# Feed-forward up products of an audio tower: from one product in full fp32 to three products of split halves

## The reference

```
h = tok(x)                                  # projection, layer norm, 5-tap conv with soft gates, W_ff, relu
h = h + attn(layernorm(h), w_qkv, w_o)      # 8 heads of 64
h = h + ffn(layernorm(h), up, down, perm)

def ffn(x, up, down, perm):                 # up [16, 64, 256], down [16, 256, 64]
    t = x.reshape(b * l, 1024)[:, perm].reshape(b * l, 16, 64)
    t = einsum('bhd,hdm->bhm', t, up)       # the up products: K is 64
    t = gelu(t, approximate=False)
    t = einsum('bhm,hmd->bhd', t, down)     # the down products: K is 256
    return t.reshape(b * l, 1024)[:, unperm]
```

## Time and profile before

| | us |
|---|---|
| median of 3 runs | 996.25 (995.29 to 996.93) |
| the profiled execution, its time | 1000.3 |
| the same, span from first to last instruction | 997.8 |
| PE busy | 959.8 (96%) |
| DVE busy | 507.4 (51%) |
| ACT busy | 426.6 (43%) |
| POOL busy | 401.4 (40%) |
| feed-forward stage, first up product to end of span | 860.0 to 997.8 |

### The profile page before, as it was taken

How to read it: one execution, slowest core, us unless ns; L and a number is a source line. 1 busy time by engine, 2 the same in 40 slices (tenths; PEclk the granted TensorE clock), 3 DMA queues, 4 the chain that set the end, 5 groups by cost and what they waited for, 6 DMA issues and landing times.

```text
span 997.8 us, 15717 instructions
## 1 busy us (share of the span) xinstructions
PE 959.8 (96%) x6108; PEld 713.8 (72%) x6108; DVE 507.4 (51%) x841; ACT 426.6 (43%) x756; POOL 401.4 (40%) x324
## 2 busy tenths in 40 slices
PE   7999999999999799999999999999999999999996
PEld 5777878777777688788778878878887877533331
DVE  6144444478545610454466256257154468759451
ACT  6144444464552542444444244234232232467553
POOL 1124242435651113535352352342023278668632
PEclk9899999999999999999999999999999999999999
DMA  8550908286345225418300300200024976724521
GB/s 287 199 203 1 184 34 176 61 151 170 127 138 153 92 43 162 139 64 302 120 11 12 106 2 21 106 1 22 29 81 157 265 264 235 272 92 127 175 79 63
DMA packets 74919, 122.87 MB, mean 123 GB/s; under 512 B 29143, under 2 KB 38359, under 8 KB 70878
## 3 DMA queue, kind: packets, MB, share of 16 engines
q1 hardware_dynamic: 68686, 104.93, 35.0%
q0 software_dynamic: 5120, 16.78, 4.9%
q10 hardware_dynamic: 1040, 0.16, 0.1%
HBM read 79.36 MB, written 42.50 MB: 122 GB/s over the span
## 4 chain that ended last, share of the span: by engine, by line
PE 79%; DVE 5%; POOL 5%; issue 4%; ACT 3%; DMA 2%; SPq 0%; POOLq 0%; ACTq 0%; DVEq 0%
PE bank L333 20%; PE bank L334 19%; PE bank L335 19%; PE bank L1848 6%; PE bank L1857 6%; POOL vacc L369 2%; DMA stage<-w_proj 2%; POOL wf_l L327 2%; DVE yr_l L1197 2%; PE bank L1600 2%; DVE sq L414 1%; ACT sq L419 1%; PE bank L1730 1%; PE bank L435 1%; ACT yr_h L857 1%
## 5 line engine op out<-in xcount | busy, mean ns | idle before, releaser
L369 POOL TENSOR_TENSOR vacc<-vacc,sq 128x512 f32<-128x512 f32 x72 | 96.8, 1344 | 41.6 <-ACT sq L419 28.3
L333 PE MATMUL bank<-xa_h,wp_h 128*128 128x512 f32 x256 | 104.1, 406 | 7.1 <-DVE xa_l L1148 7.1
L333 PE MATMUL bank<-cv_h,wf_h 128*128 128x512 f32 x256 | 104.9, 410 | 4.1 <-DVE lg L1212 2.4
L334 PE MATMUL bank<-xa_l,wp_h 128*128 128x512 f32 x256 | 101.8, 398 | 0.0
L335 PE MATMUL bank<-xa_h,wp_l 128*128 128x512 f32 x256 | 101.7, 397 | 0.0
L334 PE MATMUL bank<-cv_l,wf_h 128*128 128x512 f32 x256 | 100.5, 393 | 0.0
L335 PE MATMUL bank<-cv_h,wf_l 128*128 128x512 f32 x256 | 100.4, 392 | 0.0
L1129 ACT ACTIVATE gt<-bank 128x512 f32<-128x512 f32 x128 | 66.2, 602 | 54.1 <-PE bank L1848 54.0
L735 POOL TENSOR_TENSOR fo<-fo,res 128x512 f32<-128x512 f32 x32 | 42.3, 1337 | 112.6 <-ACT fo L881 69.6
L1848 PE MATMUL bank<-dd,up_f 64*128 64x512 f32 x256 | 64.9, 625 | 0.4 <-ACT gt L1129 0.4
L397 POOL TENSOR_TENSOR acc<-acc,ho 128x512 f32<-128x512 f32 x24 | 34.2, 1424 | 72.4 <-ACT ho L852 70.1
(11 more groups left out here) (178 smaller groups left out, 2173.7 us busy)
## 6 DMA issues: line engine op xcount, KB each, us to landing
xs<-x_t SPq DMA_DIRECT2D x32, 256.0 KB, 6.2
h_s<-ho SPq DMA_DIRECT2D x8, 1024.0 KB, 5.0
res<-h_s SPq DMA_DIRECT2D x32, 256.0 KB, 3.6
h_s<-fo SPq DMA_DIRECT2D x32, 256.0 KB, 2.4
dc<-h_s SPq DMA_DIRECT2D x4, 2048.0 KB, 8.9
h<-h_s SPq DMA_DIRECT2D x8, 1024.0 KB, 8.1
h_s<-h SPq DMA_DIRECT2D x8, 1024.0 KB, 5.3
band_s<-zero SPq DMA_DIRECT2D x4, 1072.0 KB, 8.5
```

Of the source, the lines that this page charges most:

```text
L333: pe.matmul(o, wh, xh, start=start, stop=False)
L334: pe.matmul(o, wh, xl, start=False, stop=False)
L369: g.tensor_tensor(vacc[:, :], t[:, 0, :] if k == 1 else vacc[:, :], t[:, at, :], ALU.add).then_inc(ln_vac, 1)
```

## The change

The operands of the up products are split as those of the other stages, and `ff_up` makes three passes.

- `up` is loaded raw; ACT makes its high part in two copies of 128x1024 and DVE the low part in place, in two subtractions, both at the end of o chunk c = 2.
- Each block of the input gets a high part from ACT (`xd_high`, in a ring of RING = 4 tiles), three steps ahead, behind the gelus of a step, and a low part from DVE (`xd_low`) that overwrites the scaled block, two steps ahead, behind `d_add`. DVE makes the low parts of blocks 0 and 1 in the o stage, ahead of its last two evacuations.
- `ff_up` now has six float32r products for each `blk` where it had two in float32, and waits for `xd_lo` in place of `xd_sc`.
- Two semaphores are added (`xd_hi`, `xd_lo`), and the ring of raw weight loads goes from 9 to 7.

```diff
-        up_f = place("up_f", [P, KB, FF_MID], F32, R1)
+        up_h = place("up_h", [P, KB, FF_MID], F32R, R1)
+        up_r = place("up_r", [P, KB, FF_MID], F32, R1 + 8 * KIB)
+        up_l = place("up_l", [P, KB, FF_MID], F32R, R1 + 8 * KIB)
+        dd_h = place("dd_h", [P, RING, N], F32R, STAGE)
+        dd_l = place("dd_l", [P, KB, N], F32R, R2 + 48 * KIB)
...
+                if c == CH - 2:
+                    act.wait_ge(up_ld, 32)
+                    for i in range(2):
+                        act.activation(up_h[:, 4 * i:4 * i + 4, :], up_r[:, 4 * i:4 * i + 4, :], ACT.Copy).then_inc(w_hi, 1)
+            def xd_high(b):
+                act.wait_ge(xd_sc, b + 1)
+                if b >= RING:
+                    act.wait_ge(up_mm, 4 * (b - RING) + 4)
+                act.activation(dd_h[:, b % RING, :], dd[:, b % KB, :], ACT.Copy).then_inc(xd_hi, 1)
+            for b in range(RING - 1):
+                xd_high(b)
...
                 gelus(s // KB, s % KB)
+                if s + RING - 1 < CH * KB:
+                    xd_high(s + RING - 1)
...
+            def xd_low(b):
+                v.wait_ge(xd_hi, b + 1)
+                v.tensor_tensor(dd_l[:, b % KB, :], dd[:, b % KB, :], dd_h[:, b % RING, :].bitcast(F32),
+                                ALU.subtract).then_inc(xd_lo, 1)
...
                     o_low(c + 1, range(PAIRS - 1))
+                else:
+                    xd_low(0)
+                    xd_low(1)
                 o_evac(c, A_GROUPS[2])
...
+                if c == CH - 2:
+                    for i in range(2):
+                        half = slice(4 * i, 4 * i + 4)
+                        v.wait_ge(w_hi, U_END + i + 1)
+                        v.tensor_tensor(up_l[:, half, :], up_r[:, half, :], up_h[:, half, :].bitcast(F32),
+                                        ALU.subtract).then_inc(w_lo_v, 1)
...
                     d_add((s - 1) // KB, (s - 1) % KB)
+                if s + 2 < CH * KB:
+                    xd_low(s + 2)
...
-                    since(pe, xd_sc, c, 8, a + 1)
+                    since(pe, xd_lo, c, 8, a + 1)
...
+                b = (8 * c + a) % RING
                 for j, r in enumerate(halves):
-                    mm = pe.matmul(bank[2 * blk + j][:, :], up_f[r, a, cols], dd[r, a, :], start=True, stop=True)
+                    pe.matmul(bank[2 * blk + j][:, :], up_h[r, a, cols], dd_h[r, b, :], start=True, stop=False)
+                for j, r in enumerate(halves):
+                    pe.matmul(bank[2 * blk + j][:, :], up_h[r, a, cols], dd_l[r, a, :], start=False, stop=False)
+                for j, r in enumerate(halves):
+                    mm = pe.matmul(bank[2 * blk + j][:, :], up_l[r, a, cols], dd_h[r, b, :], start=False, stop=True)
...
-            pe.wait_ge(up_ld, 32)
+            pe.wait_ge(w_lo_v, lo_before[0][U_END] + 2)
...
+RING = 4
+
-RAW = 9
+RAW = 7
```

More of the change, by code:

```diff
@@ L205, in audio_tower @@
         d_ld, d_cent = [sem(f"d_ld{i}") for i in range(2)], sem("d_cent")
-        xd_sc, up_ld = sem("xd_sc"), sem("up_ld")
+        xd_sc, xd_hi, xd_lo, up_ld = (sem(s) for s in ("xd_sc", "xd_hi", "xd_lo", "up_ld"))
         g_ld = [[sem(f"g_ld{i}{k}") for k in range(KB)] for i in range(2)]
@@ L649, in _ @@
             for s in range(2):
-                sp.dma_start(up_f[FF_IN * s:FF_IN * (s + 1), :, :],
+                sp.dma_start(up_r[FF_IN * s:FF_IN * (s + 1), :, :],
                              up.rearrange("(a s) d m -> s d a m", s=2)[s]).then_inc(up_ld, 16)
```

## The result

The changed kernel takes 1001.29 us (median of 20 runs, 996.95 to 1008.48), the kernel before in the same comparison 996.48 (20 runs). The ratio is 1.0049, 95% interval 1.0032 to 1.0067: slower by 4.9 us where 4.9 less was forecast. The prediction was wrong in sign. One run far slower than all others, of 1347.28 in experiment 8, is left out of its times.

A forecast was written before the change was run, and what follows sets the result against it. PE was taken as the bound, with less room in steps 8 to 14. Terms -11.5 + 3.3 + 0.4 + 1.6 + 1.3 = -4.9 took 996.25 to 991.4, overall range 987 to 998.5.

The forecast's parts named there:

- the clock: Behind the variance product: left unchanged; a second half-clock stretch at the start would cost 1.7, chance 0.07 with DVE's waits.
- the ring: Smaller ring of weight loads: last load and `c_load(1)` 2.3 later, costing PE about 1.3, nothing more at POOL's sum; bounds 0 and 4.
- the table loads: Behind ACT's two table loads in the feed-forward a copy stands in front of the gelus, costing 0.4.
- The up products: Feed-forward on PE: six slots of 0.227 a step, each step saves 0.36, 32 steps save 11.5.
- Rival 1: Every slot of `ff_up`: float32r weight loads at 64 rows not hidden, nothing saved, time 999.2; chance 0.11.
- Steps 15 to 31 all have this length: Kernel before, feed-forward on PE: each of these steps takes 3.78.
- ACT: High copies in the feed-forward: 0.3 behind per step with squares, costing nothing alone but leaving no room for DVE's lateness.
- DVE against POOL: Steps 8 to 13: DVE's low parts, held by POOL's additions, give back 3.3 to PE; bounds 0 and 5.
- The pass of 3.8: DVE in steps 8 to 11: six operations and a short wait take 3.8 a step, before POOL's holds.
- the five holds of 0.95: Steps 8 to 13: POOL's additions hold DVE five times for about 0.95 each.
- rival 2: DVE, POOL, start and ring give back nearly all, only the steps behind 15 gain; time 996, chance 0.20.
- The start: Start of the feed-forward: low parts ahead of the last evacuations make PE begin 1.6 later; bounds 0.7 and 3.7.

The follow-up runs named there:

- experiment 8: Changed kernel with ring of nine, blocks 6 and 7 prepared later, last centrings spread out and their mean read from PSUM; ratio 0.9991, 995.4.
- 9: The ceiling: changed kernel with ring of nine, no low part of the blocks on DVE, second pass reading the high part; ratio 0.9920, 8.0 under before.
- 2: The ring-of-nine kernel: changed kernel with the ring of raw weight loads back at nine; ratio 1.0029, +2.9 against the kernel before.
- experiment 10: Changed kernel with ring of nine, POOL's additions for the last two variances on 8 of 512 columns; ratio 0.9932, 989.5.
- psum_center: The kernel of experiment 6: changed kernel with ring of nine, last eight centrings reading their mean from PSUM; ratio 0.9996, 995.9.
- best2: Changed kernel with ring of nine, both variances' centrings reading the mean from PSUM, DVE's start reordered with blocks 6 and 7 in steps 0 and 1; 0.9950, 991.3.
- 7: Kernel before (ring of nine, float32 up products) with the blocks' copies, subtractions and PE's waits added, results unused; ratio 1.0072, +7.2.
- 3: Changed kernel (ring of seven) with the last centrings spread over steps 8 to 14 and the variance product moved to step 16; ratio 1.0039, +3.9.
- 5: Changed kernel with ring of nine, low parts of blocks 0 and 1 ahead of the evacuations, blocks 6 and 7 prepared behind them; ratio 1.0010, +1.0.
- experiment 6: Same run as psum_center: changed kernel with ring of nine, last eight centrings reading their mean from PSUM instead of SBUF; ratio 0.9996, 995.9.
- 4: Changed kernel (ring of seven) without DVE's low parts for blocks 2 to 31, the second pass reading the high part; ratio 0.9974, 993.7.
- experiment 1: Kernel before with only the ring of raw weight loads cut from nine to seven; ratio 1.0032, +3.2.

## Why the prediction was wrong

Two steps of the prediction failed. It put the clock at nothing ("I leave this as it is"), where the feed-forward has 10.2 us at half clock for 3.4 before, up to 3.4 us of cost, and the ring another stretch of 3.4, up to 1.7. And it put the low parts beside POOL at 3.3, where PE's waits behind the start sum to 5.3. At full clock the feed-forward was to be 6.2 shorter (-11.5 + 3.3 + 0.4 + 1.6) and is 1.8 shorter.

By measured times the 4.9 are -8.0 for the products (9), +10.9 for what the low parts do to DVE and the clock (from 9 to 2), +2.0 for the ring (from 2 to the changed kernel), each within about 3. Forecast were -11.1 (with the table loads), +4.9 and +1.3.

- **The up products: right in mechanism, 0.9 too much in size.** The slot is 0.232 instead of 0.227, a step saves 0.33, 32 steps 10.6. Rival 1 is dead: loads of 64 rows are hidden. ("Steps 15 to 31 all have this length" holds from 16 on; step 15 of before took 5.43, with the stretch of the earlier trace rows in it, which changes no sum.) The 8.0 of the ceiling is less, since there too PE waits.
- **ACT: right, but for a path that it left out.** ACT's copies beside the squares cost PE nothing in experiment 10, as forecast. What PE waits for in the ceiling (1.3 for gelus) is DVE's preparation, held by POOL and handed on through ACT's order: a high copy that waits 1.91 for its block holds the gelus behind it. The changed kernel has it too (0.58 at 908.50, there through a square that waits 1.50 for a centring), and psum_center (1.71 and 0.62) and best2 (1.42 and 0.63) have it most. The prediction said that ACT "leaves no room for DVE's lateness" and gave about 1 for squares; the copy as a second such place isn't in its sum.
- **DVE against POOL: right in mechanism, 2.0 too small.** Behind the start PE waits 0.48 + 0.71 + 0.58 + 1.53 + 2.02 = 5.3 in the changed kernel, over the 3.3 forecast and over its bound of 5. The pass of 3.8 was right (3.74 without POOL's time), the five holds of 0.95 weren't: in steps 9 to 11 a hold lasts 1.5, a whole POOL addition, in every pass, and the passes take 5.2 to 5.7. Experiments 7 and 10 settle it: 5.24 with PE's old step, 3.74 without POOL's time. PE can't gain anything where DVE's pass is longer than even its old step and DVE's lead is used up, and steps 1 to 4 were so too (passes of 4.0 to 4.5), which I had left out: the waits of 0.48 and 0.71 stand right behind them. Experiments 3, 5 and 8 show that order alone moves the waits and doesn't remove them. Removing the second SBUF input (6) frees the centrings, yet at full clock that is worth 0.7, because the preparation and low parts are held in their place; removing POOL's time (10) removes the waits.
- **The clock: put at nothing, and the larger error in kind.** "I leave this as it is; a second such stretch at the start would cost 1.7" was put with rival 2's waits into a rest of 0.07, 998 to 1000, the forecast nearest to what came. The ring-of-nine kernel has 10.2 of half-clock in the feed-forward, the ceiling 0; over all their runs the difference is 10.0. That is 3.1 to 5.1 of the 10.9, by the two prices above. Every profiled kernel that waited 1.9 to 2.6 for a low part ahead of its first up product (after, 2, 3, 4, 6, 10) had a stretch of 3.4 or 6.8 right behind it; 5, 8, 9 and 11, which wait under 0.4 there, had none, nor 1 with 1.0 and 7 with 1.3. PE's waits for DVE were priced at their own length, and not at what the clock does behind them.
- **The start: 1.6 forecast, 2.7 in the trace of after** (3.0 between the stages against 0.32), 1.9 with the ring of nine. Within its bounds.
- **The ring: mechanism right, size off.** `c_load(1)` is 2.5 later (2.3 forecast), PE loses 2.2 and not 1.3 in experiment 1, since POOL's sum was late by 1.1 on top, which I had ruled out. In the changed kernel it is 2.4, all of it in the one gap of 2.18 and what follows it directly, with nothing added at POOL's sum. Why the same delay splits in one kernel and not in the other is open.
- **Rival 2 had the right shape** (nearly all given back, by DVE, POOL, start and ring), but ended at 996, for want of the clock.

The Trainium skill ("SBUF — State Buffer", section "SBUF: two separate sides") says that the lock between DVE and POOL holds for a DVE operation with two SBUF inputs against a POOL operation that reads SBUF. Experiment 6 agrees: with one input in PSUM no centring was held, 0.69 or less, where the same centrings had taken 2.1. I had used the rule for the price of a hold, but not to ask which operations hold whom.

What stays open: why the half-clock stretch comes where it comes. Of the eight waits of 1.7 to 2.1 inside the feed-forward (all kernels) only three were followed by one within 2 us: 2.02 in the changed kernel, 2.00 in late_prep and 1.86 in dve_only, but not 2.00 in ring9_after, 2.04 in spread, 1.87 in combined, 1.77 in best2 or 1.71 in psum_center. The kernel before has one behind its second variance product and ring7_before none there. No run isolates it, so that PE's waits cause the extra half-clock time is argued from these traces, not shown.

## What to carry to other kernels

Price work added to a half-idle engine by the stretch where that engine is fullest, as a pass length against the step of the bounding engine, with each of POOL's additions beside it added in full where DVE's operation reads two inputs from SBUF; where the pass is longer than the old step, the whole gain of these steps is gone. Follow a late operation also through the engines that run in order: here DVE's lateness reached PE by way of ACT's gelus too. A wait of about 2 us on PE may cost more than itself, since a half-clock stretch of 3.4 can follow; it did in 6 of 6 cases at the start and in 3 of 8 later, so carry it as a range. A DVE operand that already lies in PSUM can be read there and takes the operation out of POOL's way, but the hold then falls on the next operation that reads SBUF twice.

## What the hardware showed that was not expected

- DVE operations with a PSUM operand (`hg<-bank,hg` x32: 677 to 693 ns in the changed kernel) were never held by POOL in any run here; those with two SBUF operands took up to 2.3 us.
- Two back-to-back POOL additions took 2.98 beside DVE, and a pair of centrings beside them (2.80 instead of 1.28) stood for the whole of one.
- Time at PE's lower clock in the feed-forward went from 0 to 10.2 us between kernels that differ little in their waits, up to 5.1 us of cost.
